# Attention values times probabilities: the low part stored in the high part's zero rows, two products in place of three

## The reference

```python
s = attention(xn)          # 32 query heads, 8 key/value heads, head size 128, rope,
                           # key j allowed for query i if j <= i and j > i - 128
g = silu(ffn(xn))          # 512 -> 1376 -> 512, gated, 4-bit weights with scales
out = x + s * g
# in the attention, per head:
scores = where(allowed, q @ k.T * 128 ** -0.5, lowest)
attn = softmax(scores)
out_h = attn @ v ; s = concat(out_h) @ wo
```

## Time and profile before

| what | value |
|---|---|
| median of 3 runs | 802.13 us (802.11 to 802.34) |
| profiled execution, its own time | 802.26 us |
| span, first to last instruction | 800.4 us |
| TensorE busy | 796.0 us, 99% |
| VectorE busy | 567.4 us, 71% |
| GpSimd busy | 475.2 us, 59% |
| ScalarE busy | 428.5 us, 54% |

### The profile page before, as it was taken

The page is one execution under the profiler, slowest core; times in us unless marked ns, Lnnn a source line. Parts: engine busy times, 40 slices in busy tenths (PEclk is TensorE's granted clock), DMA queues, the critical chain, the costliest instruction groups (busy, mean ns, idle before and its releaser), DMA issues.

```text
span 800.4 us, 13468 instructions
## 1 busy us (share of the span) xinstructions
PE 796.0 (99%) x3966; PEld 672.4 (84%) x3966; DVE 567.4 (71%) x1634; ACT 428.5 (54%) x1104; POOL 475.2 (59%) x357
## 2 busy tenths in 40 slices
PE   9999999999999999999999999999999999999998
PEld 7888888888888888888888888888888888888887
DVE  7715867668448867767686777778677777867785
ACT  5413313223138675666666566666656566665672
POOL 2103314224256774867487486748757674878997
PEclk9999999999999999999999999999999999999999
DMA  9659525201000400400040040004004000420102
GB/s 282 187 178 269 139 67 158 77 29 53 1 27 14 132 14 1 132 2 14 2 131 13 0 131 0 13 0 131 13 0 131 0 13 0 131 66 0 40 0 106
DMA packets 51908, 54.00 MB, mean 67 GB/s; under 512 B 4128, under 2 KB 33184, under 8 KB 51872
## 3 DMA queue, kind: packets, MB, share of 16 engines
q1 hardware_dynamic: 51728, 53.50, 22.6%
q10 hardware_dynamic: 144, 0.07, 0.0%
HBM read 47.25 MB, written 6.29 MB: 67 GB/s over the span
## 4 chain that ended last, share of the span: by engine, by line
PE 93%; POOL 4%; issue 2%; ACT 0%; DVE 0%; POOLq 0%; ACTq 0%
PE bank L1349 26%; PE bank L1350 26%; PE bank L1351 26%; PE bank L1540 3%; PE bank L1556 3%; PE bank L1573 2%; PE bank L1574 2%; PE bank L1575 2%; PE bank L1582 1%; POOL swap L457 1%; PE bank L1579 1%; PE bank L1580 1%; PE bank L1478 1%; POOL acc L488 1%; POOL q L461 1%
## 5 line engine op out<-in xcount | busy, mean ns | idle before, releaser
L457 POOL TENSOR_TENSOR swap<-swap,cst 128x512 f32<-128x512 f32 x80 | 107.9, 1349 | 41.7 <-ACT swap L701 41.7
L722 ACT ACTIVATE probs<-probs,nmx 128x128 f32<-128x128 f32 x256 | 100.0, 392 | 59.9 <-DVE nmx L1123 59.8
L1349 PE MATMUL bank<-xh,wih 128*128 128x512 f32 x320 | 128.9, 403 | 0.0
L1350 PE MATMUL bank<-xl,wih 128*128 128x512 f32 x320 | 125.2, 391 | 0.0
L1351 PE MATMUL bank<-xh,wil 128*128 128x512 f32 x320 | 125.0, 391 | 0.0
L1349 PE MATMUL bank<-woh,oh 128*128 128x512 f32 (+1 forms) x260 | 100.9, 388 | 0.0
L1350 PE MATMUL bank<-wol,oh 128*128 128x512 f32 (+1 forms) x260 | 100.6, 387 | 0.0
L1351 PE MATMUL bank<-woh,ol 128*128 128x512 f32 (+1 forms) x260 | 100.5, 387 | 0.0
L405 POOL TENSOR_TENSOR hl<-act_h,hh 128x512 fp32r<-128x512 f32 x22 | 31.6, 1436 | 99.6 <-ACT hh L603 99.6
L461 POOL TENSOR_TENSOR q<-q,swap 128x512 f32<-128x512 f32 x64 | 86.0, 1344 | 6.6 <-DVE q L1098 1.6
L480 POOL TENSOR_TENSOR ph<-ph,cst 128x512 fp32r<-128x512 f32 x32 | 41.8, 1305 | 73.3 <-ACT ph L737 73.3
(11 more groups left out here) (140 smaller groups left out, 2026.9 us busy)
## 6 DMA issues: line engine op xcount, KB each, us to landing
raw<-in_wq SPq DMA_DIRECT2D x32, 256.0 KB, 4.6
raw<-in_wo SPq DMA_DIRECT2D x32, 256.0 KB, 5.0
pk<-in_w SPq DMA_DIRECT2D x44, 128.0 KB, 3.6
sc<-in_s SPq DMA_DIRECT2D x44, 128.0 KB, 3.8
vals<-stage SPq DMA_DIRECT2D x16, 256.0 KB, 2.8
vraw<-vals SPq DMA_DIRECT2D x16, 256.0 KB, 2.9
pk<-in_w SPq DMA_DIRECT2D x11, 256.0 KB, 2.7
sc<-in_s SPq DMA_DIRECT2D x11, 256.0 KB, 3.1
```

The source lines that it names most:

```text
L457: nc.gpsimd.tensor_tensor(v, v, spread(sin.unsqueeze(1), P, 2, SEQ), ALU.mult).then_inc(sin_done, 1)
L722: e = nc.scalar.activation(probs[:, s, c0:c1], probs[:, s, c0:c1], ACT.Exp, bias=nmx[:, s, i:i + 1], scale=-1.0, accum_out=rsum[:, s, i:i ...
L1349: nc.tensor.matmul(out_, sh, mh, start=(i == 0), stop=False)
L1350: nc.tensor.matmul(out_, sh, ml, start=False, stop=False)
```

## The change

For t = 0 the early queries (columns 0 to 63 of each head) see only keys 0 to 63 of their tile, so the rows 64 to 127 of their high part are zero. The same holds for the kept triangle. The low part of these columns is now written into those rows of `ph`. The values of keys 0 to 63 stand twice in a new tile `vtwice` (rows 0 to 63 and again 64 to 127), so one product over 128 rows gives high x high and high x low together; a second one, over 64 rows, adds low values x high probabilities. The late queries keep their three products, on 256 columns (4 heads x 64). So one attend has three matmuls of 512 columns and ten of 256, two of them over 64 rows, in place of nine of 512. `v_hi` makes two copies more, `p_hi` of r = 1 one copy of 64 rows, `p_lo` is split for r = 0 and has a second part for r = 1, and `near` has three operations of half the columns, with a second mask `keep_twice`.

```diff
         def near(g, bp, b):
+                late = spread(keep[:, HALF:P].unsqueeze(1), P, GH, HALF)
+                early = spread(keep_twice[:, 0:HALF].unsqueeze(1), P, GH, HALF)
+                pool.wait_ge(ph_done, cnt(4, g, bp, 2 * b + 2))
+                wait(pool, o_ps, cnt(4, g, bp, 2 * b))
+                nc.gpsimd.tensor_tensor(late_q(ph[:, 2, :]), late_q(ph[:, 1, :]).bitcast(f32), late,
+                                        ALU.mult).then_inc(kept, 1)
+                pool.wait_ge(pl_done, cnt(4, g, bp, 2 * b + 2))
+                nc.gpsimd.tensor_tensor(late_q(pl[:, 2, :]), late_q(pl[:, 1, :]).bitcast(f32), late,
+                                        ALU.mult).then_inc(kept, 1)
+                pool.wait_ge(early_hi, cnt(2, g, bp, b + 1))
+                pool.wait_ge(early_lo, cnt(2, g, bp, b + 1))
+                nc.gpsimd.tensor_tensor(early_q(ph[:, 2, :]), early_q(ph[:, 2, :]).bitcast(f32), early,
+                                        ALU.mult).then_inc(kept_early, 1)
...
             def v_hi(g, bp):
-                nc.scalar.activation(vh[:, bp, :, :], vraw[:, bp, :, :], ACT.Copy).then_inc(vh_done, 1)
+                nc.scalar.activation(vh[:, bp, :, :], vraw[:, bp, :, :], ACT.Copy)
+                first_rows = vraw[0:HALF, bp, :, :]
+                nc.scalar.activation(vtwice[0:HALF, bp, :, :], first_rows, ACT.Copy)
+                nc.scalar.activation(vtwice[HALF:P, bp, :, :], first_rows, ACT.Copy).then_inc(vh_done, 1)
...
             def p_hi(g, bp, b, r):
                 nc.scalar.activation(ph[:, r, :], T_B[r][:, :], ACT.Copy).then_inc(ph_done, 1)
+                if r == 1:
+                    act.wait_ge(ph_done, cnt(4, g, bp, 2 * b + 2))
+                    nc.scalar.activation(early_q(ph[0:HALF, 2, :]), early_q(ph[0:HALF, 1, :]).bitcast(f32),
+                                         ACT.Copy).then_inc(early_hi, 1)
...
             def p_lo(g, bp, b, r):
                 dve.wait_ge(ph_done, cnt(4, g, bp, 2 * b + r + 1))
+                if r == 0:
+                    nc.vector.tensor_tensor(late_q(pl[:, 0, :]), late_q(T_B[0][:, :]),
+                                            late_q(ph[:, 0, :]).bitcast(f32), ALU.subtract)
+                    nc.vector.tensor_tensor(early_q(ph[HALF:P, 0, :]), early_q(T_B[0][0:HALF, :]),
+                                            early_q(ph[0:HALF, 0, :]).bitcast(f32), ALU.subtract).then_inc(pl_done, 1)
+                    return
                 nc.vector.tensor_tensor(pl[:, r, :], T_B[r][:, :], ph[:, r, :].bitcast(f32),
                                         ALU.subtract).then_inc(pl_done, 1)
+                nc.vector.tensor_tensor(early_q(ph[HALF:P, 2, :]), early_q(T_B[1][0:HALF, :]),
+                                        early_q(ph[0:HALF, 1, :]).bitcast(f32), ALU.subtract).then_inc(early_lo, 1)
...
             def p_turn(g, bp, b, r, end=False):
+                if r == 1:
+                    wait(pe, early_lo, cnt(2, g, bp, b))
...
             def attend(g, bp, b, end=False):
+                    if t == 0:
+                        o_early, o_late = early_q(O_B[j % 2][:, :]), late_q(O_B[j % 2][:, :])
+                        nc.tensor.matmul(o_early, vtwice[:, bp, 2 * b, :], early_q(both_h), start=True, stop=False)
+                        nc.tensor.matmul(o_early, vl[0:HALF, bp, 2 * b, :], early_q(ph[0:HALF, 0, :]),
+                                         start=False, stop=True)
+                        nc.tensor.matmul(o_late, near_h, late_q(both_h), start=True, stop=False)
+                        nc.tensor.matmul(o_late, near_h, late_q(both_l), start=False, stop=False)
+                        nc.tensor.matmul(o_late, near_l, late_q(both_h), start=False, stop=True).then_inc(o_ps, 1)
+                        continue
                     nc.tensor.matmul(O_B[j % 2][:, :], near_h, both_h, start=True, stop=False)
                     nc.tensor.matmul(O_B[j % 2][:, :], near_h, both_l, start=False, stop=False)
+                    nc.tensor.matmul(O_B[j % 2][:, :], near_l, both_h, start=False, stop=False)
+                    step_h, step_l = [v[:, bp, 2 * b + 1, :] for v in (vh, vl)]
+                    pe.wait_ge(kept, cnt(4, g, bp, 2 * b + 1))
+                    o_early, o_late = early_q(O_B[j % 2][:, :]), late_q(O_B[j % 2][:, :])
+                    nc.tensor.matmul(o_late, step_h, late_q(ph[:, 2, :]), start=False, stop=False)
+                    nc.tensor.matmul(o_late, step_l, late_q(ph[:, 2, :]), start=False, stop=False)
+                    pe.wait_ge(kept, cnt(4, g, bp, 2 * b + 2))
+                    nc.tensor.matmul(o_late, step_h, late_q(pl[:, 2, :]), start=False, stop=False)
+                    pe.wait_ge(kept_early, cnt(2, g, bp, b + 1))
+                    nc.tensor.matmul(o_early, vtwice[:, bp, 2 * b + 1, :], early_q(ph[:, 2, :]), start=False, stop=False)
+                    nc.tensor.matmul(o_early, vl[0:HALF, bp, 2 * b + 1, :], early_q(ph[0:HALF, 2, :]),
+                                     start=False, stop=True).then_inc(o_ps, 1)
```

More of the change, by code:

```diff
@@ L45 @@
 ALL_Y = NT * NKV
-C_COS, C_SIN, C_MASK, C_ID, C_W = 0, SEQ, 2 * SEQ, 2 * SEQ + 4 * P, 2 * SEQ + 5 * P
+C_COS, C_SIN, C_MASK, C_ID, C_W = 0, SEQ, 2 * SEQ, 2 * SEQ + 5 * P, 2 * SEQ + 6 * P
 def build(nc, x, wq, wk, wv, wo, w13, s13, w2, s2, const, shifts, out):
@@ L70, in build @@
         cos, sin = cst[:, C_COS:C_COS + SEQ], cst[:, C_SIN:C_SIN + SEQ]
-        causal, plain, far, keep = [cst[:, C_MASK + n * P:C_MASK + (n + 1) * P] for n in range(4)]
+        causal, plain, far, keep, keep_twice = [cst[:, C_MASK + n * P:C_MASK + (n + 1) * P] for n in range(5)]
         ident = cst[:, C_ID:C_ID + P]
@@ L124, in build @@
         vl = sb("vl", [P, 2, IT // P, HD], f32r, main)
+        vtwice = sb("vtwice", [P, 2, IT // P, HD], f32r, main)
         pace = sb("pace", [P, 4 * GH], f32, main)
@@ L175, in build @@
         vh_done, vl_done, kept = sem("vh_done"), sem("vl_done"), sem("kept")
+        early_hi, early_lo, kept_early = sem("early_hi"), sem("early_lo"), sem("kept_early")
         pT_ps, ph_done, pl_done = sem("pT_ps"), sem("ph_done"), sem("pl_done")
@@ L236, in second, with early_q, late_q @@
             return ap.rearrange("p (b t n) -> p b t n", b=2, t=2)[:, :, 1, :]
+        def early_q(ap):
+            return ap.rearrange("p (h t n) -> p h t n", h=GH, t=2)[:, :, 0, :]
+        def late_q(ap):
+            return ap.rearrange("p (h t n) -> p h t n", h=GH, t=2)[:, :, 1, :]
         def spread(ap, *sizes):
@@ L1573, in attend @@
                     nc.tensor.matmul(O_B[j % 2][:, :], near_h, both_h, start=True, stop=False)
                     nc.tensor.matmul(O_B[j % 2][:, :], near_h, both_l, start=False, stop=False)
[L1575 to L1582, removed]
@@ L1583, in attend @@
-                    m.then_inc(o_ps, 1)
+                    nc.tensor.matmul(O_B[j % 2][:, :], near_l, both_h, start=False, stop=False)
[4 more added lines that the diff above has]
+                    nc.tensor.matmul(o_late, step_l, late_q(ph[:, 2, :]), start=False, stop=False)
@@ L1720, in constants @@
     i, j = np.arange(P)[:, None], np.arange(P)[None, :]
-    for n, block in enumerate((np.where(j <= i, 0.0, NEG), np.zeros((P, P)), j > i, i <= j)):
+    for n, block in enumerate((np.where(j <= i, 0.0, NEG), np.zeros((P, P)), j > i, i <= j, i % HALF <= j)):
         c[:, C_MASK + n * P:C_MASK + (n + 1) * P] = block
```

## The result

| | before | after |
|---|---|---|
| median | 802.35 us (802.11 to 802.54, six runs) | 823.21 us (823.02 to 824.18, six runs) |
| profiled execution, span | 802.26, 800.4 us | 823.02, 821.2 us |

The ratio is 1.0261 (95%: 1.025 to 1.0272). The kernel became slower by 20.9 us, where 5.3 us faster was predicted.

The account below looks back on a forecast made before the run. TensorE was taken as the bound, busy throughout the middle stage, so only fewer column-starts save time. -5.9 + 1.0 - 0.4 = -5.3 us, from 802.13 to 796.8 us; range 795 to 818.

Parts of the forecast that it names:

- TensorE's columns: Each attend's matmuls take 1.856 us instead of 2.04, saving 0.184 us a call, 5.9 us for 32.
- The lag of 0.03: 512-column matmuls start wider apart after a run of 256-column ones: 0.03 us for each of 32 attends, 1.0 us lost.
- pieces of columns: Early and late queries as four 64-column pieces in TensorE's moving operand cost as one piece; upper bound 35 us.
- The change of rows: TensorE going from 128 rows to 64 and back, 128 changes in all, was taken to cost nothing.
- rival 1: Around each attend's 64-row matmuls, row changes empty the array: 817.7 us (chance 0.13), or 831.7 with loads exposed (0.07).
- the break-even of 0.041: Price in us of one change of rows on TensorE at which the kernel would be neither faster nor slower.
- The upper bound's parts: Per change of rows on TensorE: 0.163 us of lost overlap, plus 0.11 for a late weight load, 0.27 together.
- A gain beside it, 0.4 us: In the last stage, TensorE's waits on the kept low part shrink as GpSimd finishes sooner; bounds 0 and 0.5.
- GpSimd: Three 128x256 multiplications replace two of 128x512, 0.8 us each, 2.4 in all, leaving 0.2 us to spare.
- rival 3: GpSimd's 256-column multiplications exceed 0.87 us, so the early product waits in 16 attends; up to 20.2 us, 817; chance 0.08.
- ScalarE, `v_hi`'s copies, "Cost 0": Two added 64x512 copies of some 0.60 us delay `exps` and `halves` up to 0.8 us, hidden by idle time.
- VectorE, "Cost 0": Added `p_lo` work, 0.5 us an attend, 17 us in all, fits in 130 us free in the middle stage.

Follow-up runs that it names:

- e1: The changed kernel with both 64-row products taken over all 128 rows; 810.48 us, ratio 1.010 to the kernel before.
- e2: The changed kernel with the two 64-row products put side by side in the first attend of each step; 820.61 us, ratio 1.0227 to the kernel before.
- e5: e1 with ScalarE's two `vtwice` copies moved behind `halves(ng, nbp, 2)`, with their own semaphore; 800.35 us, ratio 0.9973 to the kernel before.
- e7: The kernel before with only the two `vtwice` copies added in `v_hi`, read by nothing; 807.95 us, ratio 1.0069.
- e6: e1 with VectorE's second `p_lo` part for r = 1 cut to one column in all groups but the first; 809.13 us, ratio 1.0083 to the kernel before.
- e9: e5 with ScalarE's `o_hi(g, bp, 2)` put ahead of `kq_hi(ng, nbp, 3)`; 797.80 us, ratio 0.9944 to the kernel before.

## Why the prediction was wrong

**TensorE's columns: right.** 1.856 us plus 0.03 was forecast for an attend, 1.88 measured in e1. Three matmuls of 512 columns and ten of 256 did save 0.16 us a call when all had 128 rows. The lag of 0.03 and "pieces of columns" at the price of one piece (0.12) held as well.

**The change of rows: the step that failed.** "I take nothing, since the nearest rows, the changes of kind, show no gap." It measured 0.195 us a change at 256 columns and 0.19 at 512, 25 us in all, so the term put at nothing is larger than the whole gain. The price lies between those of rival 1, 0.163 and 0.273, near the lower, and 823.2 falls between that rival's 817.7 and 831.7. Rival 1 named the right place, the sign to watch for (starts 0.2 us or more apart beside the 64-row matmul) was the right one, and so was the break-even of 0.041; the choice below it was not. The reason given, that transposes and f32/fp32r changes leave no gap, compared the wrong thing: all those rows are 128*128, so none of them says anything about another row count. Where the trace has no row of a kind, an absence of gaps elsewhere should have weighed little.

The Trainium skill (TensorEngine Tiling (Array Packing), Key Properties) says that changing the tiling mode drains the engine, and this case agrees with a price for each change, 0.19 us at 64 and at 32 rows and next to none at 96. Whether the array is drained in full no row shows. Its rule was cited as rival 1 and, as it turned out, given too small a chance.

**The upper bound's parts.** "If the array had to finish one matmul before the next enters" 0.163, and the exposed load 0.11 on top. The pair in e2 shows both parts: 0.09 ahead of the first matmul of another row count, where 0.163 was drawn, and 0.10 to 0.11 behind it, where 0.11 was. A matmul on 64 rows starts at 440.59, while the record of the one before runs to 440.66, so by the (modelled) records the array had not finished; what happens inside it stays open.

**A gain beside it, 0.4 us: right in size, with help.** The two late kept products of the last stage lost 0.5 us before and nothing in the changed kernel, whose row changes gave GpSimd time; in e5, without them, 0.3 us of waits are left there. Three small waits near 774 to 777 us, 0.3 together, went too. Against it stand the 1.1 us of waits on GpSimd elsewhere.

**GpSimd: nearly right.** 0.8 forecast, 0.739 measured for the two late operations (0.70 start to start). The early one, L497, has the same in most of its records and 1.18 us in some, a mean of 0.842. In the second attend of the second step, the spot that the prediction had timed, the third operation ended at 457.80 and its product started at 458.68, so rival 3 did not come to pass there. Nor did it in e5, where no row change gave it time: only two attends of the last stage waited for the third operation, 0.15 and 0.17 us. The small waits came in the second attend of the other step, whose rows the prediction did not read: there GpSimd itself idles 0.96 us for VectorE's `p_lo`, so that it is not its own speed that is late.

**ScalarE, `v_hi`'s copies, "Cost 0": wrong, though it did not show in the time.** Alone they cost 5.5 us (e7), and in e1 10.1 (by e5). The prediction read the idle time right behind the copies and the next reader of the bank that `cos_part` frees, and had the delay of `halves` right (up to 0.8 us; measured 0.75). It did not follow VectorE's queue on from `cos_part` to `p_lo`, nor GpSimd's to the kept low part, which had less slack than that: the 1.09 us of idle time that it counted as cover (1.23 in the step that matters) was not cover but the start of the chain. No rival named it.

**VectorE, "Cost 0": small.** With one of its two added operations cut to one column 1.35 us come back, at the waits behind `ol` (e6).

**The likeliest case** would have been 796.8; with 128 rows, the copies moved and one `o_hi` earlier, e9 takes 797.8. The range of 795 to 818 missed 823.2: it stopped at the lower price of rival 1, where the bound drawn for a change reached 0.273. One small slip stands in the chances: rival 3 gives half of its 0.08 to "faster", and the sum there uses 0.03. It changes nothing.

## What to carry to other kernels

Don't put a lone matmul over 64 or 32 rows among matmuls over 128: pad it to 96 or 128 rows, or put all the short ones side by side, as each visit costs as much as three more matmuls of 256 columns (all of it measured in this kernel's fp32r mode). When work is added to an engine's queue, follow what it delays through the other engines' queues to the next thing that TensorE waits for; idle time just behind the addition is no cover when the engine behind it starts an unbroken run at that point. For an operation that no row shows, let the bounds set the chance rather than rows of another kind.

## What was not expected of the hardware

A visit to 64 rows costs 0.39 to 0.40 us whether the matmul has 256 or 512 columns, and 32 rows cost the same; with 96 rows an attend is 0.03 us longer and the kernel the same. Two visits merged into one cost 0.12 us for the second matmul, as any other.

Around a change of row count the weight load stood at its own matmul's start (440.59, 440.90) and not 0.22 us ahead of it. The Trainium skill (TensorE: Matmul & The Clock Gate, Step-by-step: what each phase is for) says that weights are pulled ahead of a running matmul when the row groups don't conflict or the spare weight buffer is the target. Across the change that did not happen in either direction; between two matmuls of the same row count it did, with 128 rows (441.01 for 441.12) and with 64 (442.39 for 442.51).

A GpSimd multiplication of 128x256 took 0.739 us, 0.57 of the 1.29 us for 128x512. And the idle times and the busy share of TensorE hid 25 us: a matmul on a new row count got a longer record (0.38 for 0.28) in place of a gap.
